# Last batch of both attentions: scores and exponentials in six parts, and one batch's router rows moved to the end

## The chip, the cores and the metric

The kernel runs on one core of a Trainium2 chip. The metric is device time in microseconds of one execution. Engines: PE (TensorE, matmuls and transposes; PEld is its weight load), ACT (ScalarE), DVE (VectorE), POOL (GpSimd), and SP (SyncE), which issues most DMAs. Each engine works its instructions in the order written, and semaphores tie the engines together.

## What is computed

A model of two layers over 8 batches of 256 tokens with 256 features. In each layer:

```python
x = x + tanh(g_xattn[l]) * attention_l(layernorm(x), ctx)      # 16 heads of 16
x = x + tanh(g_ffn[l])   * experts_l(layernorm(x))             # 8 experts, top 2
# attention, per batch and head
scores = q @ k.T / sqrt(16); p = softmax(scores); o = p @ v; out = o @ Wo.T + bo
# router, per token
logits = layernorm(x) @ gate_w (+ gate_b)
```

In the second layer each expert has a fixed capacity. The normalised rows of the second layernorm ("router rows") are written to memory, since the experts gather them by token.

## The kernel before

`program` runs, for each layer, `attention_phase` and then `route_and_experts`. Each is a block of its own: the second starts when every engine has ended the first. The change touches `attention_phase` alone, in both layers.

An attention works batch by batch (b = 0 to 7), software-pipelined: while PE computes the maxima of batch b+1, ACT exponentiates batch b. Per batch there are two passes over the scores. The first (`head_scores`, `take_maxima`) finds each row's maximum through the two banks `ps_max`. `max_transpose` on PE, `maxima` on ACT and `maxima_to_slots` on SP put the negated maxima as an extra row into `q_s` (semaphore `m_ld[c]`). The second pass recomputes scores with that row, so that their exponential needs no further subtraction:

- `scores(b, c)` (PE, matmuls at L1069): four heads (c = 0 to 3 are the four groups of a batch) into the four banks of `ps_st`, one head for each group of 32 rows of the array. Each is two fp32 matmuls of 256 columns, and the profile shows 16 instructions. It waits until the exponential of the group before has read `ps_st` (`prob_ready`).
- `probabilities(b, c)` (ACT, L581): one exponential over 128 x 2048 into `prob[n % 2]`, when `weigh_values` of two groups before has read that buffer (`pv_ps`).
- `weigh_values(b, c)` (PE, L1083): 16 instructions, values times probabilities, into `ps_head`.
- after two groups `heads(b, u)` (ACT, L587) copies `ps_head`, `turn_heads(b, u)` (PE, L1092) transposes it back, and `normalise(b, u)` (DVE, L777 and L781) divides by the sums into `o`.
- `o_transpose` (PE, L965 by the helper `turn`), `outputs` (ACT, L575), `outputs_low` (DVE, L829) and `out_project` (PE, L89 to L91) project it, and `residual` (DVE, L787) adds it to x.
- `router_moments` (DVE, L795 and L798), `router_scale` and `router_rows` (POOL, L402 to L414; for batch 7 the rows are DVE's, L807) give the normalised rows `xr`. `store_router_rows` on SP writes them out. `router_turn` (PE, L965), `router_inputs` (ACT, L563), and `router_logits` (PE L993, DVE L817 or L819) give the logits.

`o_transpose`, `out_project`, `router_turn` and `router_logits` all share the bank `ps_lin`, so their order is fixed by waits.

The order on each engine is written out by hand, at the end of its part of the block. Around batches 6 and 7 it is a list without loops (PE from L1283 on). `fill_first` and `fill_last` are transposes of `ident` into a bank nobody reads (L98), which keep PE busy while it would wait. In the first attention `project_later(0)` to `(2)` stand there in part: projections for the second layer into `ps_max` and `ps_st`, which ACT copies out by `keep_later` (L142, L144).

Of the kernel before, what the change touches and what calls it, by code (L numbers as in the profile page):

```python
# [101 lines left out]
KV_EARLY, KV_FIRST, KV_RANKED = 3, 1, 8  # L102
# [45 lines left out]
def attention_phase(nc, layer, shared, dram, early):  # L148
# [4 lines left out]
    with ExitStack() as ctx:  # L153
# [3 lines left out]
        def ps(name, shape):  # L157
            return ctx.enter_context(nc.psum_tensor(f"{name}_a{layer}", shape, F32))
# [3 lines left out]
        def sem(name):  # L162
            return new_sem(f"{name}_a{layer}")
# [20 lines left out]
        def key_columns(b):  # L184
# [10 lines left out]
        prob = [sb(f"prob{i}", [P, HG, QT, S]) for i in range(2)]  # L195
# [8 lines left out]
        xr_t = sb("xr_t", [P, KC, S])  # L204

        ps_st = ps("ps_st", [P, HG, QT, S])
        ps_max = [ps(f"ps_max{i}", [P, QT, S]) for i in range(2)]
        ps_head, ps_lin = ps("ps_head", [P, 512]), ps("ps_lin", [P, 512])


# [20 lines left out]
        gate_ld, r_stat, r_mean, r_eps, r_rstd_ready, xr_ready, xr_stored, x_stored = (  # L231
            sem(n) for n in ("gate_ld", "r_stat", "r_mean", "r_eps", "r_rstd_ready", "xr_ready", "xr_stored", "x_stored"))
        rt_ps, rt_ready, lg_ps, lg_done = (sem(n) for n in ("rt_ps", "rt_ready", "lg_ps", "lg_done"))
        later_ld, later_hi, later_split, later_home, later_ps, later_kept = (
            sem(n) for n in ("later_ld", "later_hi", "later_split", "later_home", "later_ps", "later_kept"))

        def tail_bank(u):
            bank = ps_st[:, 2, :, :] if u == 2 else ps_max[u][:, :, :]
            return bank.rearrange("p q s -> p (q s)")

        def x_tiles(b):
# [280 lines left out]
        def _(act):  # L522
# [37 lines left out]
            def router_inputs(b):  # L560
                act.wait_ge(rt_ps, b + 1)
                wait(act, lg_ps, b)
                act.activation(xr_t[:, :, :], ps_lin[:, :].rearrange("p (k s) -> p k s", k=KC), ACT.Copy).then_inc(rt_ready, 1)  # L563
# [13 lines left out]
            def probabilities(b, c):  # L577
                n = b * CH + c
                act.wait_ge(st_ps, n + 1)
                wait(act, pv_ps, n - 1)  # L580
                act.activation(prob[n % 2][:, :, :, :], ps_st[:, :, :, :], ACT.Exp, scale=HD ** -0.5).then_inc(prob_ready, 1)  # L581

            def heads(b, u):
                n = b * OCT + u
                act.wait_ge(pv_ps, 2 * n + 2)
                wait(act, turned, n - 1)
                act.activation(head_t[n % 2][:, :, :], ps_head[:, :].rearrange("p (c s) -> p c s", c=2), ACT.Copy).then_inc(head_out, 1)  # L587

            loads = {"wq": wq_ld, "wk": wk_ld, "wv": wv_ld, "wo": wo_ld}

            def weight_high(n):
# [5 lines left out]
            def keep_later(u):  # L597
                if u == 0:
                    act.wait_ge(later_ld, 48)
                    act.wait_ge(later_home, 32 * EARLY_HOMES)  # L600
                act.wait_ge(later_ps, u + 1)
                keep_projection(act, early, shared, u, tail_bank(u)).then_inc(later_kept, 1)
# [96 lines left out]
            heads(B - 2, 0)  # L699
            maxima(B - 1)  # L700
            probabilities(B - 2, 3)
            heads(B - 2, 1)
            router_inputs(B - 3)
            probabilities(B - 1, 0)
            outputs(B - 2)
            probabilities(B - 1, 1)
            probabilities(B - 1, 2)
            heads(B - 1, 0)
            probabilities(B - 1, 3)
            router_inputs(B - 2)  # L710
            heads(B - 1, 1)
            outputs(B - 1)
            if layer == 0:
                for u in range(KV_EARLY):
                    keep_later(u)
            router_inputs(B - 1)


# [1 line left out]
        def _(dve):  # L720
# [89 lines left out]
            def router_logits(b):  # L810
                if b == 0 and layer:
                    dve.wait_ge(gate_ld, 32)
                dve.wait_ge(lg_ps, b + 1)
                lg = ps_lin[:, 0:QT * E].rearrange("p (q e) -> p q e", q=QT)
                tiles = slice(b * QT, b * QT + QT)
                if layer:
                    dve.tensor_tensor(logits[:, tiles, :], lg, spread(gate_b[:, :], 1, QT), ALU.add).then_inc(lg_done, 1)  # L817
                else:
                    dve.tensor_copy(logits[:, tiles, :], lg).then_inc(lg_done, 1)  # L819
# [125 lines left out]
            residual(B - 2)  # L945
            router_moments(B - 2)
            normalise(B - 1, 0)
            router_logits(B - 2)
            normalise(B - 1, 1)
            outputs_low(B - 1)  # L950
            residual(B - 1)
            router_moments(B - 1)
            router_rows(B - 1)
            router_logits(B - 1)
            if layer == 0:
# [5 lines left out]
        def _(pe):  # L961
# [17 lines left out]
            def router_turn(b):  # L979
                wait_routed(pe, b)  # L980
                if b < 4:
                    wait(pe, q_evac, 2 * (b + 5))
                if b >= 4:
                    wait(pe, x_done, b + 1)
                turn(xr[:, b * QT:b * QT + QT, :], ps_lin).then_inc(rt_ps, 1)

            def router_logits(b):
# [72 lines left out]
            def scores(b, c):  # L1060
# [10 lines left out]
                                        start=True, stop=True)  # L1071
                ins.then_inc(st_ps, 1)

            def weigh_values(b, c):
                n = b * CH + c
                if c % 2 == 0:
                    wait(pe, o_ready, b * OCT + c // 2)
                pe.wait_ge(prob_ready, n + 1)
                if c == 0:
                    pe.wait_ge(v_done, b + 1)  # L1080
                for kt in range(QT):
                    for g in range(HG):
                        ins = pe.matmul(ps_head[32 * g:32 * g + 32, c % 2 * S:(c % 2 + 1) * S], v[b % 3][:, kt, c * HG + g, :],  # L1083
                                        prob[n % 2][:, g, kt, :], start=kt == 0, stop=kt == QT - 1)
                ins.then_inc(pv_ps, 1)
# [10 lines left out]
            def o_transpose(b):  # L1096
                pe.wait_ge(o_ready, b * OCT + OCT)
                if layer and b == 0:
                    pe.wait_ge(q_evac, 2 * 4)
                elif layer or b >= B - 3:  # L1100
                    pe.wait_ge(lg_done, b)
                else:
                    pe.wait_ge(v_done, b + 4)
                turn(o, ps_lin).then_inc(ot_ps, 1)
# [10 lines left out]
            def project_later(u):  # L1115
                if u == 0:
                    pe.wait_ge(later_split, 2)
                    pe.wait_ge(mt_ready, B)
                    pe.wait_ge(max_done, B * H)
                    pe.wait_ge(prob_ready, B * CH)  # L1120
                later_projection(pe, early, u, tail_bank(u)).then_inc(later_ps, 1)

            def fill_first(n):
                keep_busy(pe, ps_st[:, 0, 0, 0:P], ident, n)
# [2 lines left out]
                pe.wait_ge(q_evac, 2 * 3)  # L1127
                keep_busy(pe, ps_lin[:, 0:P], ident, n)

            def fill_last(n):  # L1130
                keep_busy(pe, ps_max[1][:, 0, 0:P], ident, n)

            fill_first(24)
# [149 lines left out]
            max_transpose(B - 1)  # L1283
            scores(B - 2, 3)
            turn_heads(B - 2, 0)
            fill_last(6)
            weigh_values(B - 2, 2)
            weigh_values(B - 2, 3)
            router_turn(B - 3)
            scores(B - 1, 0)  # L1290
            turn_heads(B - 2, 1)
            router_logits(B - 3)
            fill_last(3)
            o_transpose(B - 2)
            scores(B - 1, 1)
            fill_last(3)
            out_project(B - 2)
            weigh_values(B - 1, 0)
            scores(B - 1, 2)
            weigh_values(B - 1, 1)  # L1300
            fill_last(8)
            scores(B - 1, 3)
            turn_heads(B - 1, 0)
            router_turn(B - 2)
            fill_last(2)
            weigh_values(B - 1, 2)
            weigh_values(B - 1, 3)
            router_logits(B - 2)
            turn_heads(B - 1, 1)
            fill_last(6)  # L1310
            o_transpose(B - 1)
# [4 lines left out]
            out_project(B - 1)  # L1316
            if layer == 0:
                project_later(1)
                project_later(2)
                fill_first(8)  # L1320
            else:
                fill_last(31)
            router_turn(B - 1)
            if layer == 0:
                fill_first(6)
# [1012 lines left out]
```

## Time and profile before

| | us |
|---|---|
| median of 3 runs | 812.64 |
| lowest, highest | 810.8, 818.65 |
| the profiled execution | 811.17 |
| its span, first to last instruction | 809.4 |
| PE busy, share of the span | 747.7, 92% |
| DVE busy | 585.1, 72% |
| ACT busy | 467.9, 58% |
| POOL busy | 383.8, 47% |
| mean granted clock of PE | 0.971 of full speed |

Busy time is summed over the whole span. What the change is worth is read from the end of each attention, about 178 to 213 us and 649 to 683.6 us from the span's start. In the rows, times are microseconds from the span's start, a bracket gives the engine's idle time before the row and what ended it, and "x16" counts merged instructions.

### The profile page before, as it was taken

The numbers are of one execution on the slowest core, as the hardware profiler recorded it, in microseconds if no ns is written. First come the engines' busy times: TensorE is split into PE (matmuls) and PEld (weight loads), VectorE is DVE, ScalarE is ACT, GpSimd is POOL, SyncE is SP. The second block draws the span as 40 slices with busy tenths as digits, with TensorE's granted clock in tenths as the row PEclk, the third lists the DMA queues.
The fourth block names the chain that finished last, engine by engine and source line by source line (L and its number), as shares of the span: only waits on it lengthen the run. The fifth ranks groups of instructions, "written<-read, shape, count | busy, mean of one in ns | idle before, by whom it ended". The sixth has DMA issues, their size and how long they took to land. (4 is left out here: it accounts for less than half of the span.)

```text
span 809.4 us, 17221 instructions
## 1 busy us (share of the span) xinstructions
PE 747.7 (92%) x6802; PEld 630.5 (78%) x6802; DVE 585.1 (72%) x1181; ACT 467.9 (58%) x716; POOL 383.8 (47%) x375
## 2 busy tenths in 40 slices
PE   6999999999899999999999956999999998879995
PEld 5666776767899999999999955556666667869994
DVE  4777777672568998898898833877777833779972
ACT  3476766755266766676676634466667661535640
POOL 6464554132054767666666344465452130263533
PEclk9999999999999999999999997998999999889998
DMA  7010000001169888888888526000000002387742
GB/s 227 22 55 21 22 29 28 28 30 54 30 219 389 273 250 251 276 253 263 266 262 258 179 33 197 27 15 29 15 15 16 15 21 81 116 301 235 202 83 26
DMA packets 47696, 103.44 MB, mean 128 GB/s; under 512 B 9952, under 2 KB 38240, under 8 KB 39936
## 3 DMA queue, kind: packets, MB, share of 16 engines
q0 software_dynamic: 16800, 65.46, 27.5%
q1 hardware_dynamic: 30816, 36.87, 13.9%
q8 instruction: 54, 0.88, 0.4%
q14 instruction: 26, 0.21, 0.1%
HBM read 84.22 MB, written 17.83 MB: 126 GB/s over the span
## 5 line engine op out<-in xcount | busy, mean ns | idle before, releaser
L771 DVE TENSOR_REDUCE mx_a<-ps_max_a 128x2 f32<-128x512 f32 x256 | 164.2, 685 | 42.7 <-PE ps_max_a L1050 41.7
L581 ACT ACTIVATE prob_a<-ps_st_a 128x2048 f32<-128x2048 f32 x64 | 120.2, 1878 | 39.0 <-PE ps_st_a L1069 38.8
L89 PE MATMUL ps_h_e<-xe_t_e,w_e 128*128 128x256 f32 x368 | 106.1, 288 | 11.8 <-DVE xe_t_e L2130 11.8
L91 PE MATMUL ps_h_e<-xe_t_e,w_e 128*128 128x256 f32 x368 | 103.0, 280 | 0.0
L90 PE MATMUL ps_h_e<-xe_t_e,w_e 128*128 128x256 f32 x368 | 103.0, 280 | 0.0
L1050 PE MATMUL ps_max_a<-k_r_a,q_r_a 32*128 32x512 f32 x256 | 86.0, 520 | 4.5 <-DVE mx_a L771 1.4
L91 PE MATMUL ps_y_e<-w_e,h_early 128*128 128x256 f32 x312 | 86.7, 278 | 0.0
L1895 POOL DMA_INDIRECT xe_e<-normalised_weighted,token_of x53 | 63.6, 1199 | 46.1 <-DVE token_of L1751 28.3
L89 PEld LDWEIGHTS ps_h_e<-xe_t_e,w_e 128*128 128x128 f32 x368 | 70.3, 191 | 13.8 <-DVE xe_t_e L2130 13.8
L1927 POOL DMA_INDIRECT x<-y_e,token_of x39 | 66.2, 1698 | 27.3 <-ACT y_e L2001 14.2
L1069 PE MATMUL ps_st_a<-q_s_a,k_s_a 32*128 32x256 f32 x1024 | 78.7, 399 | 0.2
L402 POOL TENSOR_SCALAR r_var_eps_a<-r_mean_var_a 128x2 f32<-128x2 f32 x16 | 3.7, 229 | 157.2 <-DVE r_mean_var_a L798 157.2
L1989 ACT ACTIVATE hid_e<-ps_h_e,b_e 128x256 f32<-128x256 f32 (+1 forms) x184 | 70.7, 449 | 1.8 <-PE ps_h_e L91 1.4
L91 PEld LDWEIGHTS ps_h_e<-xe_t_e,w_e 128*128 128x128 f32 x368 | 70.0, 190 | 0.0
L90 PEld LDWEIGHTS ps_h_e<-xe_t_e,w_e 128*128 128x128 f32 x368 | 69.9, 190 | 0.0
L1083 PE MATMUL ps_head_a<-prob_a,v_a 128*32 128x256 f32 x1024 | 68.4, 389 | 0.7 <-DVE o_a L781 0.6
L2001 ACT ACTIVATE y_e<-y_raw_e,slot_weight_e 128x256 f32<-128x256 f32 x39 | 18.1, 503 | 76.7 <-DVE y_raw_e L2102 74.9
L1050 PEld LDWEIGHTS ps_max_a<-k_r_a,q_r_a 32*128 32x128 f32 x256 | 32.6, 184 | 35.4 <-DVE mx_a L771 26.3
L2085 DVE TENSOR_TENSOR h_early<-hid_e,h_early 128x512 fp32r<-128x512 f32 (+1 forms) x92 | 57.0, 619 | 3.2
L1069 PEld LDWEIGHTS ps_st_a<-q_s_a,k_s_a 32*128 32x128 f32 x1024 | 51.4, 186 | 9.8 <-issue 7.7
L91 PEld LDWEIGHTS ps_y_e<-w_e,h_early 128*128 128x128 f32 x312 | 58.6, 188 | 0.0
L2058 DVE TENSOR_TENSOR w_e<-w_raw_w,w_e 128x1024 fp32r<-128x1024 f32 x46 | 55.6, 1218 | 1.2 <-ACT w_e L1968 1.2
(315 smaller groups left out, 2089.7 us busy)
## 6 DMA issues: line engine op xcount, KB each, us to landing
w_raw_w<-L_w SPq DMA_DIRECT2D x14, 1024.0 KB, 6.3
normalised_weighted<-xr SPq DMA_DIRECT2D x16, 256.0 KB, 2.2
x_sb<-x SPq DMA_DIRECT2D x8, 256.0 KB, 4.4
ctx_raw_a<-ctx_t SPq DMA_DIRECT2D x8, 256.0 KB, 4.5
x_sb<-x SPq DMA_DIRECT2D x2, 1024.0 KB, 8.8
x<-x_sb SPq DMA_DIRECT2D x8, 256.0 KB, 2.5
later_values<-x_sb SPq DMA_DIRECT2D x8, 256.0 KB
ctx_raw_a<-later_values SPq DMA_DIRECT2D x8, 256.0 KB, 3.9
```

The source lines that it names most:

```text
L89: pe.matmul(out, lhs[0], rhs[0], start=start, stop=False)
L90: pe.matmul(out, lhs[1], rhs[0], start=False, stop=False)
L91: return pe.matmul(out, lhs[0], rhs[1], start=False, stop=stop)
L581: act.activation(prob[n % 2][:, :, :, :], ps_st[:, :, :, :], ACT.Exp, scale=HD ** -0.5).then_inc(prob_ready, 1)
L771: dve.tensor_reduce(mx[:, q, h:h + HG + 1:HG], ps_max[j][:, :, :], AX.X, ALU.max).then_inc(max_done, 1)
L1050: pe.matmul(ps_max[j][:, :, :], q_r[b % 2][r:r + 32, c, q * P:(q + 1) * P], k_r[b % 2][r:r + 32, c, :, :], start=True, stop=True).then_inc ...
L1069: ins = pe.matmul(ps_st[:, g, kt, :], k_s[b % 3][c % 2][rows, c // 2, kt * P:(kt + 1) * P], q_s[b % 3][c % 2][rows, c // 2, :], start=True ...
L1083: ins = pe.matmul(ps_head[32 * g:32 * g + 32, c % 2 * S:(c % 2 + 1) * S], v[b % 3][:, kt, c * HG + g, :], prob[n % 2][:, g, kt, :], start= ...
L1895: pool.indirect_dma_start(out=xe[b % 2][:, q, :], out_offset=None, in_=dram["xw"], in_offset=bass.IndirectOffsetOnAxis(ap=shared["token_of ...
L1927: pool.indirect_dma_start(out=dram["out" if layer else "x1"], out_offset=bass.IndirectOffsetOnAxis(ap=shared["token_of"][:, t:t + 1], axis=0),
L1989: ins = act.activation(hid[jp % 2][:, j, 0:w], ps_h[jp % RB][:, j, 0:w], ACT.Gelu, bias=b1[b % 2][:, 2 * jp + j:2 * jp + j + 1])
L2085: dve.tensor_tensor(h[b % 2][1][:, js, 0:w], hid[jp % 2][:, :, 0:w], h[b % 2][0][:, js, 0:w].bitcast(F32), ALU.subtract).then_inc(h_ready, 1)
```

## The change

`ps_max`'s two banks become one tile `ps_pair` of two banks, which can also take scores of two heads. Batch 7's four groups of scores are computed in five pieces and exponentiated in six: group 0 whole in `ps_st`; heads 0 and 1 of group 1 in `ps_pair`; heads 2 and 3 of group 1 together with heads 0 and 1 of group 2 in `ps_st` (one group of matmuls, two exponentials); heads 2 and 3 of group 2 in `ps_pair`; group 3 whole in `ps_st`. New semaphores `last_st` and `last_prob` count them. The order on PE and ACT around them is new, and so are the fills.

Batch 6's router turn, copy and logits move behind batch 7's output projection: on PE behind `out_project(7)` (first attention: around `project_later(1)` and `(2)`), on ACT behind `outputs(7)` (and the first `keep_later`), on DVE between `router_moments(7)` and `router_rows(7)`. `router_turn(6)` waits for x of batch 7, and `router_turn(7)` for the logits of batch 6.

```diff
-        ps_max = [ps(f"ps_max{i}", [P, QT, S]) for i in range(2)]
+        ps_pair = ps("ps_pair", [P, 2, QT, S])
+        ps_max = [ps_pair[:, i, :, :] for i in range(2)]
...
+            def last_probabilities(c, pair):
+
+                n = (B - 1) * CH + c
+                heads_of = slice(0, HG) if pair is None else slice(2 * pair, 2 * pair + 2)
+                src = ps_pair[:, :, :, :] if (c, pair) in ((1, 0), (2, 1)) else ps_st[:, heads_of, :, :]
+                act.wait_ge(last_st, {(0, None): 1, (1, 0): 2, (1, 1): 3, (2, 0): 3, (2, 1): 4, (3, None): 5}[c, pair])
+                wait(act, pv_ps, n - 1)
+                act.activation(prob[n % 2][:, heads_of, :, :], src, ACT.Exp, scale=HD ** -0.5).then_inc(last_prob, 1)
...
             probabilities(B - 2, 3)
+            last_probabilities(0, None)
             heads(B - 2, 1)
+            last_probabilities(1, 0)
             router_inputs(B - 3)
-            probabilities(B - 1, 0)
+            last_probabilities(1, 1)
             outputs(B - 2)
-            probabilities(B - 1, 1)
-            probabilities(B - 1, 2)
+            last_probabilities(2, 0)
+            last_probabilities(2, 1)
             heads(B - 1, 0)
-            probabilities(B - 1, 3)
-            router_inputs(B - 2)
+            last_probabilities(3, None)
             heads(B - 1, 1)
             outputs(B - 1)
             if layer == 0:
-                for u in range(KV_EARLY):
-                    keep_later(u)
+                keep_later(0)
+            router_inputs(B - 2)
+            if layer == 0:
+                keep_later(1)
+                keep_later(2)
             router_inputs(B - 1)
...
             normalise(B - 1, 0)
-            router_logits(B - 2)
             normalise(B - 1, 1)
             outputs_low(B - 1)
             residual(B - 1)
             router_moments(B - 1)
+            router_logits(B - 2)
             router_rows(B - 1)
...
+            def last_scores_whole(c):
+
+                if c == 0:
+                    pe.wait_ge(k_masked, 2 * B)
+                    pe.wait_ge(prob_ready, (B - 1) * CH)
+                else:
+                    pe.wait_ge(last_prob, 4)
+                pe.wait_ge(m_ld[c], 16 * B)
+                for kt in range(QT):
+                    for g in range(HG):
+                        ins = last_score(c, g, kt, ps_st[:, g, kt, :])
+                ins.then_inc(last_st, 1)
+
+            def last_scores_pair(c, pair):
+
+                if c == 1:
+                    pe.wait_ge(max_done, B * H)
+                    pe.wait_ge(mt_ready, B)
+                else:
+                    pe.wait_ge(last_prob, 2)
+                pe.wait_ge(m_ld[c], 16 * B)
+                for kt in range(QT):
+                    for g in range(2):
+                        ins = last_score(c, 2 * pair + g, kt, ps_pair[:, g, kt, :])
+                ins.then_inc(last_st, 1)
+
+            def last_scores_middle():
+
+                pe.wait_ge(last_prob, 1)
...
+                for kt in range(QT):
+                    for g in range(HG):
+                        ins = last_score(1 if g >= 2 else 2, g, kt, ps_st[:, g, kt, :])
+                ins.then_inc(last_st, 1)
...
             max_transpose(B - 1)
             scores(B - 2, 3)
             turn_heads(B - 2, 0)
-            fill_last(6)
+            fill_last(6, 0)
             weigh_values(B - 2, 2)
+            last_scores_whole(0)
             weigh_values(B - 2, 3)
+            last_scores_pair(1, 0)
             router_turn(B - 3)
-            scores(B - 1, 0)
             turn_heads(B - 2, 1)
             router_logits(B - 3)
-            fill_last(3)
+            last_scores_middle()
+            weigh_values(B - 1, 0)
             o_transpose(B - 2)
-            scores(B - 1, 1)
-            fill_last(3)
+            last_scores_pair(2, 1)
+            weigh_values(B - 1, 1)
             out_project(B - 2)
-            weigh_values(B - 1, 0)
-            scores(B - 1, 2)
-            weigh_values(B - 1, 1)
-            fill_last(8)
-            scores(B - 1, 3)
+            last_scores_whole(3)
             turn_heads(B - 1, 0)
-            router_turn(B - 2)
             fill_last(2)
             weigh_values(B - 1, 2)
             weigh_values(B - 1, 3)
-            router_logits(B - 2)
+            fill_last(4)
             turn_heads(B - 1, 1)
             fill_last(6)
             o_transpose(B - 1)
...
             out_project(B - 1)
             if layer == 0:
                 project_later(1)
+            else:
+                fill_last(8)
+            router_turn(B - 2)
+            if layer == 0:
                 project_later(2)
-                fill_first(8)
             else:
-                fill_last(31)
+                fill_last(8)
+            router_logits(B - 2)
+            if layer == 0:
+                fill_first(6)
+            else:
+                fill_last(14)
             router_turn(B - 1)
```

## Rows read from the trace of the kernel before

**Rows 1.** Windows: the tail of the second attention; busy us per engine, clock, DMA share, GB/s.

```profile
core 0: us, PE busy (x) PEld busy (x) DVE busy (x) ACT busy (x) POOL busy (x), PEclk, DMA share, GB/s
649.06:683.56 34.50, 31.74 (x343) 24.27 (x339) 9.77 (x29) 14.77 (x15) 7.73 (x10) 1.00 0.08 25
```

**Rows 2.** Timeline of the second attention, batch 7's first scores: start, us, engine, line.

```profile
651.92 1.93 PE L1083 MATMUL ps_head_a<-prob_a,v_a 128*32 128x256 f32 x32 [0.15 <-DVE o_a L781]
...
653.78 0.65 PE L965 MATMUL ps_lin_a<-ident,xr 128*128 128x128 f32 x4
...
654.37 1.15 PE L1069 MATMUL ps_st_a<-q_s_a,k_s_a 32*128 32x256 f32 x16
...
655.44 0.42 PEld L1092 LDWEIGHTS ps_head_a<-ident,head_t_a 128*128 128x128 f32 x4 [0.33 <-issue]
...
655.58 1.88 ACT L581 ACTIVATE prob_a<-ps_st_a 128x2048 f32<-128x2048 f32 x1 [0.51 <-PE ps_st_a L1069]
...
657.81 1.15 PE L1069 MATMUL ps_st_a<-q_s_a,k_s_a 32*128 32x256 f32 x16
```

**Rows 3.** The same timeline, from batch 6's output projection to batch 7's last heads.

```profile
659.29 0.39 PE L89 MATMUL ps_lin_a<-wo_hi_a,o_t_hi_a 128*128 128x256 f32 x1
...
660.91 1.07 PE L1083 MATMUL ps_head_a<-prob_a,v_a 128*32 128x256 f32 x16
661.02 0.75 DVE L787 SCALAR_TENSOR_TENSOR x_sb<-ps_lin_a,tanh_g,x_sb 128x512 f32<-128x512 f32 x1 [1.78 <-PE ps_lin_a L91]
...
661.91 1.15 PE L1069 MATMUL ps_st_a<-q_s_a,k_s_a 32*128 32x256 f32 x16
662.60 0.25 DVE L798 BATCH_NORM_AGGREGATE r_mean_var_a<-r_stats_a 128x2 f32<-128x6 f32 x2
...
663.13 1.88 ACT L581 ACTIVATE prob_a<-ps_st_a 128x2048 f32<-128x2048 f32 x1 [2.22 <-PE ps_st_a L1069]
...
664.90 0.59 ACT L587 ACTIVATE head_t_a<-ps_head_a 128x512 f32<-128x512 f32 x1
...
666.23 0.66 PE L1092 MATMUL ps_head_a<-ident,head_t_a 128*128 128x128 f32 x4
...
667.69 1.93 PE L1083 MATMUL ps_head_a<-prob_a,v_a 128*32 128x256 f32 x32 [0.16 <-DVE o_a L781]
...
669.55 0.97 PEld L993 LDWEIGHTS ps_lin_a<-gate_w_a,xr_t_a 128*128 128x128 f32 x8 [0.41 <-issue]
...
669.69 0.60 ACT L587 ACTIVATE head_t_a<-ps_head_a 128x512 f32<-128x512 f32 x1 [0.98 <-PE ps_head_a L1083]
```

**Rows 4.** The same timeline, from the last heads to the last logits.

```profile
670.36 0.51 PEld L1092 LDWEIGHTS ps_head_a<-ident,head_t_a 128*128 128x128 f32 x4
...
675.51 3.55 PE L98 MATMUL ps_max_a<-ident 128*128 128x128 f32 x31
675.71 0.75 DVE L787 SCALAR_TENSOR_TENSOR x_sb<-ps_lin_a,tanh_g,x_sb 128x512 f32<-128x512 f32 x1 [1.78 <-PE ps_lin_a L91]
...
678.69 0.74 DVE L807 TENSOR_SCALAR xr<-x_sb,r_mean_var_a,r_rstd_a 128x256 f32<-128x256 f32 x2 [1.16 <-POOL r_rstd_a L404]
...
680.83 1.06 PE L993 MATMUL ps_lin_a<-gate_w_a,xr_t_a 128*128 128x8 f32 x8
681.92 0.17 DVE L817 TENSOR_TENSOR logits<-ps_lin_a,gate_b_a 128x16 f32<-128x16 f32 x1 [2.49 <-PE ps_lin_a L993]
```

**Rows 5.** Windows inside the scores at 654.37, of line 1069 alone.

```profile
654.36:654.46 0.10, 0.09 (x4) 0.09 (x4) 1.00 0.00 0
...
654.72:654.88 0.16, 0.16 (x8) 0.16 (x4) 1.00 1.03 352
```

**Rows 6.** Timeline of the first attention's end.

```profile
196.84 1.93 PE L1083 MATMUL ps_head_a<-prob_a,v_a 128*32 128x256 f32 x32 [0.15 <-DVE o_a L781]
...
206.10 0.28 PE L89 MATMUL ps_st_a<-h_early,w_part_early 128*128 128x256 f32 x1
...
207.85 0.73 DVE L807 TENSOR_SCALAR xr<-x_sb,r_mean_var_a,r_rstd_a 128x256 f32<-128x256 f32 x2 [1.16 <-POOL r_rstd_a L404]
```

**Rows 7.** Windows just behind the first attention's end.

```profile
212.00:216.00 4.00, 3.00 (x14) 3.03 (x15) 2.69 (x10) 0.06 (x1) 0.00 (x0) 0.61 0.02 4
```

More of the change, by code:

```diff
@@ L233, in attention_phase @@
         rt_ps, rt_ready, lg_ps, lg_done = (sem(n) for n in ("rt_ps", "rt_ready", "lg_ps", "lg_done"))
+        last_st, last_prob = sem("last_st"), sem("last_prob")
         later_ld, later_hi, later_split, later_home, later_ps, later_kept = (
@@ L237, in tail_bank @@
         def tail_bank(u):
-            bank = ps_st[:, 2, :, :] if u == 2 else ps_max[u][:, :, :]
+            bank = ps_st[:, 2, :, :] if u == 2 else ps_pair[:, u, :, :]
             return bank.rearrange("p q s -> p (q s)")
@@ L983, in router_turn @@
                 if b >= 4:
-                    wait(pe, x_done, b + 1)
+                    wait(pe, x_done, min(b + 1 + b // (B - 2), B))
+                if b == B - 1:
+                    pe.wait_ge(lg_done, b)
                 turn(xr[:, b * QT:b * QT + QT, :], ps_lin).then_inc(rt_ps, 1)
@@ L1072, in scores, with last_score @@
                 ins.then_inc(st_ps, 1)
+            def last_score(c, g, kt, out):
+                rows = slice(32 * g, 32 * g + 32)
+                return pe.matmul(out, k_s[(B - 1) % 3][c % 2][rows, c // 2, kt * P:(kt + 1) * P], q_s[(B - 1) % 3][c % 2][rows, c // 2, :],
+                                 start=True, stop=True)
+            def last_scores_whole(c):
[22 more added lines that the diff above has]
+                pe.wait_ge(last_prob, 1)
+                pe.wait_ge(m_ld[1], 16 * B)
+                pe.wait_ge(m_ld[2], 16 * B)
+                for kt in range(QT):
+                    for g in range(HG):
+                        ins = last_score(1 if g >= 2 else 2, g, kt, ps_st[:, g, kt, :])
+                ins.then_inc(last_st, 1)
             def weigh_values(b, c):
@@ L1077, in weigh_values @@
                     wait(pe, o_ready, b * OCT + c // 2)
-                pe.wait_ge(prob_ready, n + 1)
+                if b == B - 1:
+                    pe.wait_ge(last_prob, (1, 3, 5, 6)[c])
+                else:
+                    pe.wait_ge(prob_ready, n + 1)
                 if c == 0:
@@ L1099, in o_transpose @@
                     pe.wait_ge(q_evac, 2 * 4)
+                elif b == B - 1:
+                    pe.wait_ge(x_done, b)
                 elif layer or b >= B - 3:
@@ L1119, in project_later @@
                     pe.wait_ge(max_done, B * H)
-                    pe.wait_ge(prob_ready, B * CH)
+                    pe.wait_ge(last_prob, 6)
                 later_projection(pe, early, u, tail_bank(u)).then_inc(later_ps, 1)
@@ L1128, in fill_lin, with fill_last @@
                 keep_busy(pe, ps_lin[:, 0:P], ident, n)
-            def fill_last(n):
+            def fill_last(n, free=5):
+                wait(pe, last_prob, free)
                 keep_busy(pe, ps_max[1][:, 0, 0:P], ident, n)
@@ L1318, in _ @@
                 project_later(1)
+            else:
+                fill_last(8)
+            router_turn(B - 2)
+            if layer == 0:
                 project_later(2)
-                fill_first(8)
             else:
-                fill_last(31)
+                fill_last(8)
+            router_logits(B - 2)
+            if layer == 0:
+                fill_first(6)
+            else:
+                fill_last(14)
             router_turn(B - 1)
```

## The prediction

> **What bounds the kernel now.** I first looked at where each attention ends. The tail, from the transpose of batch 7's maxima to the end of the block, is 34.5 us in the second attention. PE is busy for 31.74 of them at a granted clock of 1.00 [rows 1]. Little of that time is slack on PE, though its fills (transposes of `ident` into a spare bank) hide some. The tail of the first attention is the same code. Its rows repeat these at times 470.85 us smaller up to batch 7's `o_transpose` (the last two weighings at 667.69 and at 196.84) [rows 3, 6]. Nothing of the route stage starts before the block's end, so a shift of the last rows moves the whole time one for one.
>
> Then I read the timeline in order, to find what each step waits for [rows 2, 3]. Scores of four heads (16 matmuls in `ps_st`) are at 654.37, 657.81 and 661.91, and once more behind them. An exponential starts 1.21 us after its scores (655.58), and the next scores must wait until it has read the banks. So there is a cycle of scores, exponential, scores. The reader should see that ACT is not full in it: before the exponential at 663.13 it sat idle 2.22 us. But the last weighing (667.69) starts behind DVE's normalisation, not behind an exponential, and its 32 matmuls take 2.00 us until `heads` (669.69). Last comes a serial chain: heads, turn (670.36), projection, residual (675.71), moments, router rows on DVE (678.69), router turn, logits (680.83), and DVE's copy of them (681.92) [rows 3, 4]. The 31 fills from 675.51 to 679.06 show that PE waits there for DVE and POOL.
>
> **Unit costs on PE, start to start.** Scores 1.07 (654.37 to 655.44). One weighing 1.00 (660.91 to 661.91), 0.86 if another weighing follows (two of them 1.86, 667.69 to 669.55). Four transposes 0.4 (their loads last 0.42), or 0.59 ahead of scores (653.78 to 654.37); ACT can read them after 0.7. Router logits 0.81 (669.55 to 670.36), and I take 0.99 ahead of scores, with the same 0.18 of switching. Output projection 1.62 (659.29 to 660.91), 1.73 until DVE can read it. One fill 0.115 (3.55 us for 31). On ACT a whole exponential holds the engine 1.77 (663.13 to 664.90) and a copy of 512 columns lasts 0.60 [rows 2 to 4].
>
> **A pair of heads (new).** No row shows scores of two heads alone. Within one group of scores, the four row groups start together, in waves of four: the first stretch holds 4 matmuls and a later one 8, four of one wave and four of the next [rows 5]. With 16 matmuls that makes four waves. Each row group has 4 instructions in turn, and a pair still has 4 in each of its two row groups. So a pair costs as much as a whole group, 1.07, not half. The bounds are 0.54 (half the matmuls) and 1.07. I take 1.07, since the waves decide it. Five groups of scores in place of four add 1.07 us to PE in each attention. The Trainium skill says, in TensorEngine Tiling (Array Packing), Tiling Modes, that tiles operate independently and that 32 by 128 gives four of them. By that rule a pair leaves half of the array idle, which speaks against splitting. The waves agree with it. A count by matmuls would put the sum 1.0 us lower over both attentions.
>
> **A half exponential (new).** Between 0.94 (half of 1.88) and 1.28 (1.88 less 0.60). The line through 512 columns at 0.60 and 2048 at 1.88 gives 1.03, which I take, with 0.94 of hold. Four halves and two wholes in place of four wholes cost ACT 0.2 us more.
>
> **The order, worked through in the second attention's times.** `weigh_values(6,2)` starts at 651.92 as before. Scores (7,0) follow at 652.92 instead of 654.37, and its exponential starts at 654.13 instead of 655.58. That is the gain, 1.45 us. But in ACT's order `heads(6,1)` now stands behind that exponential (655.92), and `router_inputs(5)` behind the first half exponential (656.43), so it starts at 657.37. PE's order has `turn_heads(6,1)` (656.57) and `router_logits(5)` (658.03) ahead of the middle scores. The middle scores are therefore at 659.02, 1.21 us after the second scores of before (657.81). From there PE has no wait. Weighing is at 660.09, `o_transpose` at 661.09, the pair at 661.68, weighing at 662.75, `out_project(6)` at 663.75, the last scores at 665.37, and the turn at 666.44, before 666.23 [rows 3]. The whole exponential lead is spent. `out_project(6)` being 4.46 us late delays DVE's residual and moments of batch 6: residual at 665.48, moments done 1.83 us later at 667.31 (row 661.02 to the end of row 662.60). They stand ahead of `normalise(7,0)`, which lasts 0.75 (between the turn's result, 0.70 after 666.23, and the weighing at 667.69 there is as much) and ends at 668.06. The last two weighings start at 668.12 instead of 667.69: **+0.43**. The last exponential ends at 668.45, in time for the second of them. The freed `router_logits(6)` in front of `turn_heads(7,1)` gives almost nothing. Before it ended as `heads` did, so the turn is at 670.8 instead of 670.36.
>
> **The moved router rows.** After the last projection PE has `router_turn(6)`, which waits for the residual of batch 7 (ends at 676.89 with the delay). It starts at 676.95, ACT's copy is at 677.6 to 678.2, logits on PE at 678.30, and DVE's `router_logits(6)` 1.09 later, at 679.39 to 679.56. On DVE that stands ahead of `router_rows(7)`, which was ready at 679.12 (678.69 plus 0.43). So **+0.48**. Then PE has 14 fills behind `router_logits(6)` (678.30 plus 0.81 and 1.61 is 680.72), while the rows are ready at 680.40 (0.74 of work and 0.06 to PE). So **+0.32**. Second attention: 0.43 + 0.48 + 0.32 = 1.2 us. POOL's rows of batch 6 end near 671 and are no part of this. SP's store of them has 8 us to land.
>
> In the first attention `project_later(1)` and all of `project_later(2)` (from 206.10, 1.43 us each) stand around the turn. Turn at 206.53, second projection from 206.93 to 208.36, logits at 208.36, DVE's copy at 209.45 to 209.62. Then the router rows of batch 7 come at 209.65, not 207.85 [rows 6]: +1.8 us. ACT's two `keep_later` copies, now behind `router_inputs(6)`, end before the last router turn. The last store and the last logits both follow these rows, so both move with them.
>
> **Sum:** 1.2 + 1.8 = +3.0 us. The profiled execution took 811.17 us (span 809.4 and 1.8 around it), so 814.2 by its own time. It is 1.5 us below the median shown, 812.64. I give the forecast on the median: 815.6. With pairs at 0.54 the sum falls by 1.0, with half exponentials at either end it moves by 0.2. Two semaphores more per attention may cost up to a few tenths where they are cleared, from the 1.5 us between the last copy (682.09) and the block's end [rows 1, 4].
>
> **Rivals.**
> 1. *The exponential lead is kept (faster).* The mechanism is the wait of scores for free banks, with its place at scores (7,3). If PE reaches them as soon as the first half of (7,2) is read, at about 663.4 in my chain, the last exponential ends near 666.6 instead of 668.2, 1.6 us earlier in each attention. Against the 0.8 and 1.4 us of the moved router rows that makes 3.2 less 2.2, so 811.6. For it is the 2.22 us of ACT idle time. Against it, ten groups of PE work stand in between, and DVE's normalisation. It decides when the middle scores start before 657.8.
> 2. *No change.* The last rows of batch 7 find cover that I count as none (ready router logits, fewer fills), or the pairs cost half and ACT turns out shorter. About 0, so 812.6. For it is that PE has 77 fills' worth of slack in the tail (31 of them in one row). Against it, DVE's order is strict.
> 3. *The clock falls.* After the block's end the first attention shows a granted clock of 0.61 over 4 us [rows 7]. If the tail's new PE waits (1.1 us before the logits of batch 5) or the other phase of the route stage bring one such stretch more in each attention, PE work of 2 us takes 4: +4 on top, 819.6. For it is that fills were cut from 77 to about 66. Against it, the clock is 1.00 through all present waits. The Trainium skill, in TensorE: Matmul & The Clock Gate, on HAM oscillation, says idle gaps bring the half rate back. By that rule short waits like these would change nothing.
>
> **How the numbers follow.** Forecast (2 to 4.5 us longer) 0.58, rival 1 0.14, rival 2 0.15, rival 3 0.13. The likeliest alone gives 814.6 to 817. Rival 1 at 811.6 and rival 3 at 819.6, with a little for the spread of a median, set the range 811 to 820. One per cent is 8.1 us, about what a measurement of this kernel can tell from no change. No case reaches it alone: faster 0.01, same 0.95, slower 0.04.
>
> **What would show it.** A group of pair scores that lasts about 1.15 us. Half exponentials near 1.03. In the second attention the middle scores near 659.0 with ACT idle before the third exponential. The turn of the last heads 0.4 later than 670.4. DVE's router rows of batch 7 right behind a logits copy, 0.9 us later in the second and 1.8 in the first attention. PE's last router turn starting right behind fills in the second. It is wrong if the middle scores start before 657.8, or if the last weighing starts before 667.7.

## The result, and the profile after

The changed kernel takes 815.43 us (median of 20 runs, 813.19 to 821.53), the kernel before 812.24 (20 runs, 809.7 to 818.65). The ratio is 1.0043, with a 95% interval from 1.0025 to 1.0061. That is 3.5 us slower (2.0 to 5.0). The forecast was 3.0 us slower, 815.6. The profiled execution took 815.15 us with a span of 813.4, against 811.17 and 809.4 before.

First the second attention's tail as one stretch, from the transpose of the last maxima to the first instruction behind the block. It answers to [rows 1] (busy us per engine, clock, DMA share, GB/s).

```profile
core 0: us, PE busy (x) PEld busy (x) DVE busy (x) ACT busy (x) POOL busy (x), PEclk, DMA share, GB/s
650.38:687.37 36.99, 33.30 (x332) 24.42 (x328) 9.59 (x29) 14.72 (x17) 7.73 (x10) 0.95 0.07 23
```

It is 2.5 us longer than before (34.50), and its clock is 0.95 where it was 1.00. So there are two things to look for, waits and PE's granted clock. The first attention shows the waits alone. This is its timeline; it answers to [rows 2, 3], whose times it meets with 470.6 us added (the weighing at 181.31 against 651.92).

```profile
181.31 1.07 PE L1144 MATMUL ps_head_a<-prob_a,v_a 128*32 128x256 f32 x16 [0.15 <-DVE o_a L796]
...
182.31 1.15 PE L1093 MATMUL ps_st_a<-q_s_a,k_s_a 32*128 32x256 f32 x16
...
183.52 1.88 ACT L598 ACTIVATE prob_a<-ps_st_a 128x2048 f32<-128x2048 f32 x1 [1.66 <-PE ps_st_a L1093]
...
184.39 1.13 PE L1093 MATMUL ps_pair_a<-q_s_a,k_s_a 32*128 32x256 f32 x8
185.30 0.59 ACT L589 ACTIVATE head_t_a<-ps_head_a 128x512 f32<-128x512 f32 x1
...
185.78 1.03 ACT L598 ACTIVATE prob_a<-ps_pair_a 128x1024 f32<-128x1024 f32 x1
...
186.68 0.62 ACT L565 ACTIVATE xr_t_a<-ps_lin_a 128x512 f32<-128x512 f32 x1
...
187.35 0.97 PEld L1010 LDWEIGHTS ps_lin_a<-gate_w_a,xr_t_a 128*128 128x128 f32 x8 [0.99 <-ACT xr_t_a L565]
187.35 1.06 PE L1010 MATMUL ps_lin_a<-gate_w_a,xr_t_a 128*128 128x8 f32 x8 [0.75 <-ACT xr_t_a L565]
...
188.34 1.15 PE L1093 MATMUL ps_st_a<-q_s_a,k_s_a 32*128 32x256 f32 x16
...
189.55 1.02 ACT L598 ACTIVATE prob_a<-ps_st_a 128x1024 f32<-128x1024 f32 x1 [2.25 <-PE ps_st_a L1093]
...
194.67 1.15 PE L1093 MATMUL ps_st_a<-q_s_a,k_s_a 32*128 32x256 f32 x16
...
196.35 0.25 DVE L813 BATCH_NORM_AGGREGATE r_mean_var_a<-r_stats_a 128x2 f32<-128x6 f32 x2
196.52 0.22 DVE L792 RECIPROCAL rsum_a<-ps_head_a 128x16 f32<-128x16 f32 x1
...
197.26 1.93 PE L1144 MATMUL ps_head_a<-prob_a,v_a 128*32 128x256 f32 x32 [0.63 <-DVE o_a L796]
```

Three things are to be seen here. A pair of heads takes 1.13 us with 8 matmuls, as long as four heads with 16. The half exponentials take 1.02 to 1.03. And PE waits (0.75 in the bracket, 0.99 by its weight load's row) for ACT's copy of batch 5's router inputs at 186.68, which stands behind the exponentials. The middle scores come behind it (188.34), and ACT is idle for 2.25 us before it can exponentiate them. The last weighings start at 197.26. With the 0.25 us by which this execution reached the tail later, that is 0.17 us later than before. This is the end of the same tail; it answers to [rows 6].

```profile
208.27 0.95 PE L1010 MATMUL ps_lin_a<-gate_w_a,xr_t_a 128*128 128x8 f32 x8
...
209.26 0.17 DVE L834 COPY logits<-ps_lin_a 128x16 f32<-128x16 f32 x1 [2.27 <-PE ps_lin_a L1010]
209.35 0.73 DVE L822 TENSOR_SCALAR xr<-x_sb,r_mean_var_a,r_rstd_a 128x256 f32<-128x256 f32 x2
...
210.13 0.66 PE L980 MATMUL ps_lin_a<-ident,xr 128*128 128x128 f32 x4 [0.20 <-DVE xr L822]
```

DVE's rows of batch 7 (209.35) stand right behind the copy of batch 6's logits. Before they were at 207.85. Now the second attention, where the same steps meet a slower array (rows as above).

```profile
659.28 1.15 PE L1010 MATMUL ps_lin_a<-gate_w_a,xr_t_a 128*128 128x8 f32 x8 [0.75 <-ACT xr_t_a L565]
...
660.36 2.09 PE L1093 MATMUL ps_st_a<-q_s_a,k_s_a 32*128 32x256 f32 x16
...
662.38 1.60 PE L1144 MATMUL ps_head_a<-prob_a,v_a 128*32 128x256 f32 x16
...
670.76 1.93 PE L1144 MATMUL ps_head_a<-prob_a,v_a 128*32 128x256 f32 x32 [0.63 <-DVE o_a L796]
...
681.97 0.17 DVE L832 TENSOR_TENSOR logits<-ps_lin_a,gate_b_a 128x16 f32<-128x16 f32 x1 [1.49 <-PE ps_lin_a L1010]
682.08 0.74 DVE L822 TENSOR_SCALAR xr<-x_sb,r_mean_var_a,r_rstd_a 128x256 f32<-128x256 f32 x2
```

The middle scores took 2.09 us instead of 1.15. Two windows, around the middle scores of the second and of the first attention, tell why (the columns are those of the first fence).

```profile
660.40:664.40 4.00, 4.00 (x37) 2.19 (x36) 0.17 (x1) 1.02 (x1) 0.00 (x0) 0.61 0.01 4
```

```profile
188.30:192.30 4.00, 4.00 (x49) 2.41 (x53) 0.74 (x2) 2.22 (x3) 0.00 (x0) 1.00 0.02 4
```

The granted clock is 0.61 in the second attention and 1.00 in the first. The mean 0.61 is made of the levels 2.4 and 1.2 GHz, most of the stretch at the lower. In the kernel before, no window of 4 us in either tail was below 1.00 until the last logits.

To compare runs, I use one length for each tail: from the start of ACT's copy of the last maxima to the start of DVE's last logits copy.

| kernel | first | second | sum over before | clock in the tails |
|---|---|---|---|---|
| before | 32.24 | 32.23 | 0 | 1.00 |
| changed | 33.48 | 34.72 | +3.7 | falls in the second |

So the profiled tails account for 3.7 of the 4.0 us by which the span grew. The rest is 0.2 to 0.3 us in other places. It is not behind the last logits: from their copy to PE's next instruction in the next block it is 1.92 us in the first attention in both kernels, so the two more semaphores show no price there.

### The profile page after: what moved, and what is told of

Same layout as the page of the kernel before. It is cut to its first block and busy times, and to the rows that moved or that the text cites. A ratio compares the mean times of both kernels' runs of the same rounds, so it can differ in the third digit from the quotient of the medians.

```text
span 813.4 us, 17185 instructions
## 1 busy us (share of the span) xinstructions
PE 747.7 (92%) x6779; PEld 627.5 (77%) x6779; DVE 584.4 (72%) x1181; ACT 467.8 (58%) x720; POOL 384.8 (47%) x375
## 5 line engine op out<-in xcount | busy, mean ns | idle before, releaser
L786 DVE TENSOR_REDUCE mx_a<-ps_pair_a 128x2 f32<-128x512 f32 x256 | 164.3, 685 | 42.9 <-PE ps_pair_a L1067 41.9
L583 ACT ACTIVATE prob_a<-ps_st_a 128x2048 f32<-128x2048 f32 x56 | 105.1, 1877 | 31.9 <-PE ps_st_a L1086 31.6
L1067 PE MATMUL ps_pair_a<-k_r_a,q_r_a 32*128 32x512 f32 x256 | 86.4, 524 | 4.4 <-DVE mx_a L786 1.4
L1086 PE MATMUL ps_st_a<-q_s_a,k_s_a 32*128 32x256 f32 x896 | 70.6, 404 | 0.1
L1067 PEld LDWEIGHTS ps_pair_a<-k_r_a,q_r_a 32*128 32x128 f32 x256 | 32.8, 185 | 34.7 <-DVE mx_a L786 25.6
L1485 POOL DMA_INDIRECT w_raw_w<-L_w,block_row x25 | 24.7, 986 | 66.5 <-DVE b_e L2143 44.3
```

Of the source, the lines that this page charges most:

```text
L786: dve.tensor_reduce(mx[:, q, h:h + HG + 1:HG], ps_max[j][:, :, :], AX.X, ALU.max).then_inc(max_done, 1)
L1067: pe.matmul(ps_max[j][:, :, :], q_r[b % 2][r:r + 32, c, q * P:(q + 1) * P], k_r[b % 2][r:r + 32, c, :, :], start=True, stop=True).then_inc ...
L1086: ins = pe.matmul(ps_st[:, g, kt, :], k_s[b % 3][c % 2][rows, c // 2, kt * P:(kt + 1) * P], q_s[b % 3][c % 2][rows, c // 2, :], start=True ...
```

## The experiments

**Theories.** *Order*: what costs is the order written on each engine, PE's wait for ACT's copy, then DVE's order, then fills. *Clock*: the new waits let the clock fall, and that is the larger part. *Additive*: each of the two parts of the change has its own share of the loss.

**Six parts alone.** Batch 6's router steps are put back where they were.

```diff
             turn_heads(B - 1, 0)
+            router_turn(B - 2)
             fill_last(2)
             weigh_values(B - 1, 2)
             weigh_values(B - 1, 3)
-            fill_last(4)
+            router_logits(B - 2)
             turn_heads(B - 1, 1)
```

> Six parts of scores and exponentials as in the changed kernel, but batch 6's router turn, copy and logits left in their old places. Order theory (PE's written order decides): the turn of batch 6's rows now stands ahead of the last two weighings, while POOL has those rows only near 4.4 us later than before, because the output projection of batch 6 is late; each attention's tail grows by about 4.2 us, 8.4 in all, so 820.7. Additive theory (the six parts cost their own share of the 3.2 us and the moved rows the rest): plus 1 to 2 us, 813 to 814.

Measured 825.0 us, ratio 1.0173 (1.0149 to 1.0197): 14 us slower, more than either theory gave (the profiled execution's span is 11.8 us longer, its two tails 12.5). Its timeline in the first attention:

```profile
197.51 2.43 POOL L416 TENSOR_SCALAR xr<-x_sb,r_mean_var_a,r_rstd_a 128x256 f32<-128x256 f32 x2
...
200.00 0.76 PE L978 MATMUL ps_lin_a<-ident,xr 128*128 128x128 f32 x4 [3.91 <-POOL xr L416]
...
201.11 3.25 PE L1140 MATMUL ps_head_a<-prob_a,v_a 128*32 128x256 f32 x32
```

and one window of it:

```profile
202.00:204.00 2.00, 2.00 (x28) 0.93 (x20) 0.00 (x0) 0.00 (x0) 0.00 (x0) 0.54 0.23 77
```

PE waits 3.91 us at the router turn for POOL's rows, with the last weighings behind it. They start 4.35 us later than before in the first attention and 4.70 in the second. Then the clock is 0.54, and the two weighings take 3.25 us instead of 1.93. Both tails show it, and they are 5.7 and 6.8 us longer than before. So the order theory's 4.2 per tail was met, and a fall of the clock behind the wait came on top. The additive theory falls: in this order on PE, with batch 6's router turn ahead of the last two weighings, the six parts are only usable together with the move.

**The move alone.** The old scores and exponentials, with batch 6's router steps at the end.

```diff
             turn_heads(B - 1, 0)
-            router_turn(B - 2)
             fill_last(2)
             weigh_values(B - 1, 2)
             weigh_values(B - 1, 3)
-            router_logits(B - 2)
+            fill_last(4)
```

(and the same lines as in the change behind `out_project(B - 1)`, on ACT and on DVE)

> The old four exponentials with only the router rows of batch 6 moved to the end. Order theory: DVE's copy of batch 6's logits stands ahead of the router rows of batch 7, and fills overshoot in the second attention; plus 1.2 us in the first attention and 0.8 in the second, 814.2. If the whole loss of the change came from the six parts, this run would be at 812.2; if it came from the move alone it would be at 815.4.

Measured 814.7, ratio 1.0039 (1.0025 to 1.0054), 3.2 us. The tails are 33.32 and 32.98, so +1.1 and +0.75, as the order theory gives. The interval, 2.0 to 4.4 us, excludes zero and overlaps the changed kernel's 2.0 to 4.9. Its lower end is a little above the 1.8 us of the tails. The profiled execution itself was 2.0 us longer than that of the kernel before (span 811.4 against 809.4), which fits the tails. Where the rest of the median's 3.2 us lies is not known.

**Middle scores first.**

```diff
             turn_heads(B - 2, 1)
-            router_logits(B - 3)
             last_scores_middle()
+            router_logits(B - 3)
```

> The changed kernel with the middle scores ahead of the logits of batch 5 on PE. Order theory: PE no longer waits 1.0 us ahead of the middle scores, the last weighings start 0.9 us sooner; 1.7 us less than the changed kernel over both attentions. Clock theory (the 1 us wait of PE lets the granted clock fall at the middle scores of the second attention, where they took 2.09 us instead of 1.15): the clock stays at 1.00 there, and another 1 to 1.5 us go, so 2.7 to 3.2 less, near the kernel before or under it.

Measured 812.83, ratio 1.0011 (0.9988 to 1.0034). Tails 32.67 and 32.36, together 0.6 us over before, with the clock at 1.00 in both. Its first attention:

```profile
185.96 0.65 PE L1153 MATMUL ps_head_a<-ident,head_t_a 128*128 128x128 f32 x4
186.54 1.15 PE L1093 MATMUL ps_st_a<-q_s_a,k_s_a 32*128 32x256 f32 x16
...
187.62 1.06 PE L1010 MATMUL ps_lin_a<-gate_w_a,xr_t_a 128*128 128x8 f32 x8
```

The middle scores follow the turn at once, 1.8 us sooner than in the changed kernel, and the logits fit behind them without a wait. The last weighings start 0.8 us sooner, since the 1 us of the logits is now behind the middle scores. One swap of two lines takes back most of the loss. It takes away the wait and, with it, whatever the clock does behind it, so alone it does not weigh the two.

**Router rows first, fewer fills.**

```diff
-            router_logits(B - 2)
             router_rows(B - 1)
+            router_logits(B - 2)
...
             router_logits(B - 2)
             if layer == 0:
                 fill_first(6)
             else:
-                fill_last(14)
+                fill_last(8)
```

> The changed kernel with batch 7's router rows ahead of batch 6's logits copy on DVE, and 8 instead of 14 fills behind batch 6's logits in the second attention. Order theory: 0.6 us less in each attention, 1.2 in all against the changed kernel, 814.2; the clock at the middle scores is not touched and may fall as before. Clock theory: only the order's 1.2 us or less, since what is left lies at the middle scores.

Measured 813.91, ratio 1.0034 (1.0022 to 1.0046). Tails 33.06 and 34.11: 0.4 less than the changed kernel in the first attention, where the last turn now starts right behind the six fills, with the rows and the logits' copy ready before it, and 0.6 less in the second, where the clock fell again at the middle scores.

**The changed kernel again.**

> The changed kernel once more. Both theories: a ratio near 1.004. Clock theory: if the fall of the clock at the middle scores of the second attention belongs to this kernel, it is there again (the scores take about 2.1 us instead of 1.15, the last weighings start 19.75 us behind the last maxima) and not in the first attention (18.17). If it was chance, the second attention's weighings start 18.2 us behind as well.

Measured 815.55, ratio 1.0026 (1.0001 to 1.0051), so 2.1 us slower than the kernel before in this second comparison, with an interval from 0.1 to 4.1. This profile, in the second attention, shows no fall:

```profile
661.34 1.06 PE L1010 MATMUL ps_lin_a<-gate_w_a,xr_t_a 128*128 128x8 f32 x8 [0.75 <-ACT xr_t_a L565]
662.32 1.15 PE L1093 MATMUL ps_st_a<-q_s_a,k_s_a 32*128 32x256 f32 x16
...
682.49 0.17 DVE L832 TENSOR_TENSOR logits<-ps_lin_a,gate_b_a 128x16 f32<-128x16 f32 x1 [1.49 <-PE ps_lin_a L1010]
682.60 0.73 DVE L822 TENSOR_SCALAR xr<-x_sb,r_mean_var_a,r_rstd_a 128x256 f32<-128x256 f32 x2
...
683.87 0.60 PE L980 MATMUL ps_lin_a<-ident,xr 128*128 128x128 f32 x4
```

The wait is the same 0.75, and the scores behind it take 1.15. The tails are 33.50 and 33.18. These are the costs of the order alone, 1.26 and 0.95, or 2.2 us.

**A later tail.** 15 more fills in the second attention behind the transpose of the last maxima.

```diff
             max_transpose(B - 1)
+            if layer:
+                fill_last(15, 0)
             scores(B - 2, 3)
```

> The changed kernel with 15 more fills behind the transpose of batch 7's maxima, in the second attention alone; they put its whole tail 1.7 us later and change no wait of PE. Wait theory (the 1.0 us wait alone lets the clock fall): the fall is still there, 1.7 us more than the changed kernel, 817.1. Moment theory (it also counts where in time the wait lies, since the first attention with the same wait shows no fall): the fall is gone, so 1.7 less 1.4, and the time is within 0.5 us of the changed kernel's 815.4.

Measured 816.92, ratio 1.0056 (1.0032 to 1.008). The clock is 1.00 through both tails, the second is 34.81 long, 1.63 over the run above, which is the price of the fills. By itself it neither confirms nor refutes that the moment decides, since the run above, of the unshifted kernel, had no fall either.

**Both repairs.** Middle scores first on PE, router rows first on DVE, 8 fills.

```diff
             turn_heads(B - 2, 1)
-            router_logits(B - 3)
             last_scores_middle()
+            router_logits(B - 3)
...
-            router_logits(B - 2)
             router_rows(B - 1)
+            router_logits(B - 2)
...
-                fill_last(14)
+                fill_last(8)
```

> The changed kernel with both repairs: the middle scores ahead of the logits of batch 5 on PE; batch 7's router rows ahead of batch 6's logits copy on DVE; 8 fills instead of 14. Order theory: plus 0.2 in the first attention and minus 0.3 in the second against the kernel before, so no difference, ratio 1.000 with no fall of the clock in the tails. If something else in the six parts costs time, it stays above 1.002.

Measured 812.75, against 812.91 of before; ratio 0.9986 (0.996 to 1.0011). Tails 32.26 and 31.71, 0.5 us under before. These are the shortest tails of all, and the time can't be told from that of the kernel before. The profiled execution shows how little one execution's whole time says here: it took 814.95 us with these tails, because its second tail began 474.3 us after its first, against 470.85 in the kernel before. Those 3.5 us lie in code that the change doesn't touch.

**Before, without fills.** The 3, 3 and 8 fills between the last batch's scores are taken out of the kernel before.

```diff
             router_logits(B - 3)
-            fill_last(3)
...
             scores(B - 1, 1)
-            fill_last(3)
...
             weigh_values(B - 1, 1)
-            fill_last(8)
             scores(B - 1, 3)
```

> The kernel before without the 14 fills (3, 3 and 8) between the last batch's scores, so that PE waits up to about 1 us there. Order theory: the fills only hide waits, no difference. Clock theory: the waits let the clock fall in the second attention's tail, plus 1 to 1.5 us, ratio 1.001 to 1.002, with scores or weighings at about twice their time in the profile.

Measured 812.83, ratio 0.9998 (0.9975 to 1.0021). Tails 32.22 and 32.23, clock 1.00 in both, although PE now waits there, once as long as in the changed kernel:

```profile
666.68 1.15 PE L1069 MATMUL ps_st_a<-q_s_a,k_s_a 32*128 32x256 f32 x16 [1.09 <-ACT prob_a L581]
```

So those fills cover waits and cost nothing, and the clock theory's extra did not show in the one profiled execution, that is in two tails.

**Router inputs first on ACT.**

```diff
             heads(B - 2, 1)
-            last_probabilities(1, 0)
             router_inputs(B - 3)
+            last_probabilities(1, 0)
```

> The changed kernel with ACT's copy of batch 5's router inputs ahead of the first half exponential. Order theory: PE's wait ahead of batch 5's logits falls from 1.0 to 0.4 us, everything behind it comes 0.6 us sooner, so 1.2 us less over both attentions than the changed kernel. If the exponentials of ACT bounded this stretch and not PE's order, holding the first half exponential back by 0.5 us would cost as much as it gains, no difference to the changed kernel.

Measured 814.57, ratio 1.0023 (0.9999 to 1.0047), which does not exclude no change. The first attention has

```profile
186.18 0.60 ACT L565 ACTIVATE xr_t_a<-ps_lin_a 128x512 f32<-128x512 f32 x1 [0.26 <-PE ps_lin_a L980]
186.68 1.02 ACT L598 ACTIVATE prob_a<-ps_pair_a 128x1024 f32<-128x1024 f32 x1
186.83 1.06 PE L1010 MATMUL ps_lin_a<-gate_w_a,xr_t_a 128*128 128x8 f32 x8 [0.20 <-ACT xr_t_a L565]
```

PE's wait goes from 0.75 to 0.20, the half exponential is 0.9 us later (6.7 us behind the last maxima in the changed kernel, 7.6 here), and the tails are 32.93 and 32.63: 0.57 and 0.55 less than with the order of the change. The exponential of the pair can wait, and the copy can't.

**Two more executions of the changed kernel.**

> One look at the changed kernel, for the clock in the tails. Waits of PE identical to the runs before; if the fall of the clock in the second attention's tail is chance of the execution, some looks have it (tail of 34.7 us from the last maxima to the last logits copy) and some don't (33.2).

> One more look at the changed kernel, as the one before: 34.7 us of tail in the second attention with a fall of the clock, 33.2 without; the first attention 33.5 in both, or about 35 if the fall comes there too.

The first: 815.25 us, tails 33.50 and 34.75, with the fall in the second attention. The second: 816.2 us, tails 35.09 and 33.18, with the fall in the *first*. So it belongs to neither attention. These are two windows of the first execution, in its second attention, and one of the second execution, in its first attention.

```profile
657.00:661.00 4.00, 3.25 (x30) 2.51 (x30) 0.86 (x3) 2.24 (x4) 0.00 (x0) 0.89 0.00 0
661.00:665.00 4.00, 4.00 (x40) 2.16 (x34) 0.00 (x0) 1.41 (x2) 0.00 (x0) 0.69 0.01 4
```

```profile
188.00:192.00 4.00, 4.00 (x37) 1.99 (x37) 0.17 (x1) 1.02 (x1) 0.00 (x0) 0.57 0.02 4
```

PE was busy 3.25 of 4 us in the stretch with the wait, and the clock fell at its end. The executions without a fall have the same 3.25 in that stretch.

Of the changed kernel's order around the middle scores there are seven profiled executions (changed, again, later tail, router rows first, six parts alone and these two), so 14 tails, each with the same wait of 0.75 us. Four have a fall behind it, and each is 1.5 to 1.6 us longer for it. The six other kernels have no such wait at that place and no fall in 12 tails, the one without fills in spite of its waits of 1.09. Every fall seen in a tail lay right behind a wait of PE. That this wait makes a fall likelier is still not quite shown: four falls would all land in the 14 tails by chance once in 15 times.

## Why the prediction was right

- *The unit costs.* The pair was taken at 1.07 us start to start for the reason of the waves. It is 1.06 (184.39 to the turn behind it), with 1.13 to its last matmul. The half exponential, 1.03, is 1.02 to 1.03. The trace agrees with the rule of the Trainium skill (TensorEngine Tiling (Array Packing), Tiling Modes) that tiles operate independently: four tiles or two take the same time.
- *The lead that is lost.* The middle scores were put at 659.02 in the times of before. They are at 658.94 (188.34 with 470.6 added), and the last scores at 665.27 against 665.37. Two runs show the cause: with the logits out of the way (middle scores first) or their input earlier (router inputs first) the tails shrink by 0.8 and 0.55 us each.
- *The first term was too large.* I gave 0.43 us for the last weighings and carried it to the turn of the last heads. It is 0.17 at the weighings and 0.06 at DVE's work behind the turn (its reciprocal at 200.60, before at 200.29, with 0.25 us between the executions). Of the 0.26 at the weighings, 0.10 is that the residual of batch 6 came sooner than in my chain, 0.08 that DVE's reciprocal (196.52) starts before the end of the aggregate (196.60) instead of behind it, and 0.07 that the normalisation is shorter. And before the change the turn stood behind `router_logits(6)`, so that its removal gave back a little, which I had taken for almost nothing.
- *The second and third terms.* 0.48 and 0.32 in the second attention measured 0.47 and 0.42 (changed kernel again: rows of batch 7 0.53 late, last logits 0.95 late). In the first attention 1.8 measured 1.26. Of the difference 0.37 is the first term again, 0.1 is DVE's rows starting 0.09 after the start of the copy ahead of them instead of after its end.
- *Which part costs.* With 0.06 us left of it at the last projection, the split into six ended about even in the changed kernel: what the first scores gained, 1.45 us, was spent in the queues behind them. Nearly all of the 2.2 us is the moved router rows, and the move alone has 1.8.
- *The sum.* The order alone costs 1.26 + 0.95 = 2.2 us, where I had 3.0. The step that was too large is the delay of the last weighings with what hangs on it; the places of the waits were right. The fall of the clock was a rival of mine, with 4 us for it and a chance of 0.13. It is real but smaller, 1.5 us a time in 4 of the 14 tails, which over two tails adds about 0.9 to a mean (an estimate from few tails). So 2.2 + 0.9 = 3.1, and 3.5 (2.0 to 5.0) is measured. The interval holds the order's 2.2 alone as well, so the medians don't prove the clock's share; the profiled tails show it. That the forecast came so near the measured number is partly luck: the 0.8 us too much in its sum stand where the clock's share belongs. The Trainium skill's page TensorE: Matmul & The Clock Gate, in its part on HAM oscillation, ties the lower rate to idle gaps; I had written that by that rule waits this short change nothing. The measurement decides: waits of 1 us were followed by a fall in 4 of 14 tails.
- *The rival that it gets faster.* It was to be decided by middle scores before 657.8. With the middle scores first they are at about 657.1 in those times, and the tail still isn't shorter than before until the router rows are first as well. The price of the moved router rows was nearly right (0.8 and 1.4, with the move alone 0.75 and 1.1). The 1.6 us of gain was too hopeful: with the middle scores first, the last scores are at about 664.5 in those times and not at 663.4, since PE works without a pause from the middle scores on, and the last weighings start 0.65 us sooner than before.
- *The rival of no change* fell with the interval, which excludes it in both comparisons, in the second one narrowly.

What stays open: why the clock falls in some executions and not in others with the same waits. In the second attention the moment fits: the three falls are in the executions where that wait of PE ended at 658.8 to 659.3 us from the span's start, and the four without a fall (again, later tail, six parts alone, the second of the two further executions) had it end at 661.3 to 662.9. In the first attention it ended at 187.0 to 187.5 in all seven, with one fall, at 187.07, so there the moment from the span's start tells nothing. The later tail had its wait among the later ones, as two unshifted executions had, so it can't decide this alone.

## What to carry to other kernels

Before splitting work so that it starts sooner, see what short and needed step stands behind it in a queue. Here a 0.6 us copy behind 1.9 and 1.0 us exponentials used up all that the earlier exponentials had gained, and one swapped line took most of the loss back. When a step is moved to the end, look at each in-order engine for what it now stands ahead of: the copy of 0.17 us cost 0.5 and 1.2 us because its input came late. And a split over row groups of the array halved the work but not the time here: 8 matmuls in two groups took 1.13 us and 16 in four groups 1.15, with four in turn in each group both times.

## What was not expected of the hardware

- A wait of PE of about 1 us was followed, in 4 of 14 tails, by a granted clock of 0.57 to 0.69 in windows of 4 us (scores 1.63 to 2.09 us instead of 1.15), at a cost of 1.5 to 1.6 us. The wait of 3.9 us with six parts alone had it in both tails.
- A DVE instruction that doesn't depend on the one ahead starts before that one's end: the router rows 0.09 to 0.11 us after the start of a copy that lasts 0.17, the reciprocal 0.17 after the start of a row of two aggregates that lasts 0.25.
